# Layer 1 attention rewritten in unrolled slots with one rounding pass, the mask added by TensorE, maxima and differences taken from PSUM

## The reference

```python
def _dyn_quant(x):
    s = jnp.maximum(jnp.max(jnp.abs(x), axis=-1, keepdims=True) / 127.0, EPS)
    q = jnp.clip(jnp.round(x / s), -127.0, 127.0)
    return (q, s)
def _w8a8_linear(x, w, b):
    qx, sx = _dyn_quant(x)
    qw, sw = _quant_weight(w)
    y = jnp.einsum('bnc,oc->bno', qx, qw) * (sx * sw[:, 0])
    return y + b
...
q = _w8a8_linear(x, wq, bq).reshape(B, N, H, D).transpose(0, 2, 1, 3)
...
scores = jnp.einsum('bhnd,bhld->bhnl', q, k) * inv_sqrt_d + mask[:, None]
attn = jax.nn.softmax(scores, axis=-1)
o = jnp.einsum('bhnl,bhld->bhnd', attn, v)
return _w8a8_linear(o, wo, bo)
```

## Time and profile before

| | |
|---|---|
| median of 3 runs | 2271.92 us (2270.27 to 2276.45) |
| the profiled execution | 2274.25 us, its span 2272.5 us |
| layer 0, up to 1671 us | 74% of the span |
| layer 1: attention's setup | 1671.0 to 1720.4 |
| attention | 1720.4 to 1964.6 |
| setup of the feed-forward part | 1964.6 to 2030.6 |
| feed-forward part | 2030.6 to 2272.5 |
| busy over the span | PE 87%, DVE 51%, ACT 46%, POOL 44% |

### The profile page before, as it was taken

One profiled execution on the slowest core, in us unless ns is written; L12 is line 12 of the kernel. 1 busy time (PEld: TensorE's weight loads), 2 busy tenths in 40 slices (PEclk: granted clock), 3 DMA queues, 4 the chain that ended last, 5 costly groups with the idle time before them and its releaser, 6 DMA issues. The chain is left out here.

```text
span 2272.5 us, 29205 instructions
## 1 busy us (share of the span) xinstructions
PE 1969.8 (87%) x9812; PEld 1410.0 (62%) x9850; DVE 1150.6 (51%) x2272; ACT 1045.7 (46%) x2189; POOL 989.2 (44%) x902
## 2 busy tenths in 40 slices
PE   3799999999999999999989999899964677328998
PEld 2566666766666676667657777799943455323443
DVE  4344433444334444444444582333445998566886
ACT  2454444444544444544442111466612433457775
POOL 1644444434544435535311000688822555107774
PEclk9999999999999999999988999899976978659999
DMA  4100000000000000000031003588666000000000
GB/s 133 47 2 1 10 29 20 1 10 1 29 20 1 10 10 19 1 1 1 1 128 47 24 15 100 170 235 231 183 190 233 3 3 2 1 28 10 24 20 24
DMA packets 71074, 114.59 MB, mean 50 GB/s; under 512 B 7552, under 2 KB 35072, under 8 KB 70224
## 3 DMA queue, kind: packets, MB, share of 16 engines
q1 hardware_dynamic: 63760, 95.95, 12.6%
q0 software_dynamic: 7168, 16.78, 3.6%
HBM read 91.74 MB, written 22.02 MB: 50 GB/s over the span
## 5 line engine op out<-in xcount | busy, mean ns | idle before, releaser
L578 POOL TENSOR_TENSOR a_xcl<-xT,a_xch 128x512 fp32r<-128x512 f32 x64 | 82.5, 1289 | 477.5 <-ACT a_xch L447 477.5
L517 DVE TENSOR_REDUCE a_nmax<-a_S 128x1 f32<-128x192 f32 (+3 forms) x256 | 139.0, 553 | 255.2 <-PE a_S L653 252.7
L709 PE MATMUL a_A<-a_pT,a_vf 128*128 128x512 f32 (+1 forms) x448 | 234.9, 606 | 1.3 <-ACT a_pT L460 1.2
L652 PE MATMUL a_S<-a_kT,a_qT 128*128 128x288 f32 (+3 forms) x640 | 213.9, 433 | 3.0 <-ACT a_pr_even L450 1.7
L110 PE MATMUL a_A<-a_wlo,a_xch 128*128 128x512 f32 x256 | 152.6, 596 | 12.1 <-DVE a_qb L540 9.4
L450 ACT ACTIVATE a_pr_odd<-a_S,a_nmax 128x320 f32<-128x320 f32 (+1 forms) x128 | 80.9, 633 | 178.2 <-DVE a_nmax L517 176.5
L460 ACT ACTIVATE a_pT<-a_TR 128x512 f32<-128x512 f32 (+1 forms) x224 | 133.0, 594 | 61.8 <-PE a_TR L699 61.8
L652 PEld LDWEIGHTS a_S<-a_kT,a_qT 128*128 128x128 f32 x640 | 120.8, 192 | 55.1 <-issue 27.6
L450 ACT ACTIVATE a_pr_even<-a_S,a_nmax 128x192 f32<-128x192 f32 (+1 forms) x128 | 66.9, 525 | 154.3 <-DVE a_nmax L517 154.2
L671 PE MATMUL a_A<-a_wkv,xT 128*128 128x256 f32 x512 | 134.8, 386 | 0.6 <-DMA a_wkv<-in_L_xattn_wv_dram 0.6
L1308 POOL TENSOR_TENSOR e_wlo<-expert_raw,e_whi 128x1408 fp32r<-128x1408 f32 x32 | 103.5, 3255 | 68.3 <-ACT e_whi L1381 68.3
(11 more groups left out here) (370 smaller groups left out, 5186.2 us busy)
## 6 DMA issues: line engine op xcount, KB each, us to landing
ffn_raw<-in_L_ffn_w_dram SPq DMA_DIRECT2D x6, 2048.0 KB
expert_raw<-in_L_ffn_w_gate_dram SPq DMA_DIRECT2D x16, 704.0 KB
expert_raw<-in_L_ffn_w_up_dram SPq DMA_DIRECT2D x16, 704.0 KB
expert_raw<-in_L_ffn_w_down_dram SPq DMA_DIRECT2D x16, 512.0 KB
x_res<-in_x_dram SPq DMA_DIRECT2D x4, 1024.0 KB
a_raw<-in_L_xattn_wq_dram SPq DMA_DIRECT2D x4, 1024.0 KB
a_raw<-in_L_xattn_wo_dram SPq DMA_DIRECT2D x4, 1024.0 KB
xn_rows<-xg SPq DMA_DIRECT2D x16, 256.0 KB, 2.0
```

Source lines behind the costliest of these rows:

```text
L517: ve.tensor_reduce(nmax[:, s % 2, i:i + 1], pair(s, i), AX.X, ALU.max, negate=True).then_inc(s_max, 1)
L578: pool.tensor_tensor(xcl[:, t % 2], xT[:, :, tok(t)], xch[:, t % 2].bitcast(F32), ALU.subtract).then_inc(xlo_ready, 1)
L652: pe.matmul(bank[:, lo:hi], qT[:, t % 2, hq], kT[:, par(t), lo:hi], start=True, stop=hi < nk)
L709: last = pe.matmul(A[:, A_USE["V", t, 0][0]], vf[r, par(t), i], pT[r, i % 2], start=i == 0, stop=i == nkt - 1)
```

## The change

Four stages are touched.

**The attention** is written like the feed-forward part: every engine walks over 21 slots, fully unrolled, and in a slot does the steps of its order string, each for the tile of the slot plus a lead (`AHEAD`). Within the steps:

- The mask, loaded once in the setup, is added in PSUM by PE: behind each product with `kbd` comes one of the identity with the mask (S). DVE takes the 16 maxima from PSUM (M) and writes `p = SC - maximum` from PSUM (s); POOL no longer has a part in that.
- The row sums come out of the product with the values, since `vbd` has two columns of ones more (V, 66 columns for 64); DVE divides the 128 x 512 result instead of the 128 x 1024 probabilities (N).
- Scale and bias of q are applied by ACT as it copies the turned q (k, four instructions of 128x128); the row scale as it copies q out of PSUM (i).
- Rounding: ACT adds ROUND = 12582912 + 0x6600 as it scales and writes f32 (q, O). The low half of such a word is the f16 of 1536 + integer; PE turns those halves, at a step of two elements (T, U), and DVE subtracts 1536 (x, o).
- Normalisation isn't multiplied out: ACT subtracts the mean (c), and the scale of the row comes from maximum and root alone (m).
- The gate is multiplied into the scales (`gsw`) and the bias (`gbo`) in the setup; POOL adds the bias to `x` (B) and later the result (A).

**Its setup** has one DVE pass for rounding in place of two, and loads `bq`, `bo` and the mask (`mask`, 512 KB in rows of 256 bytes), all ahead of `x_res`; DVE waits for all of them before it writes `kbd`. **In the feed-forward setup** `w3` is loaded at the stage's start, no longer during the attention. **In the feed-forward stage** `xq` and `hq` are f32, and PE turns their low halves.

```diff
-MAGIC = 12582912.0
+BIG = 1536.0
+ROUND = 12582912.0 + 0x6600
+def low_half(ap):
+    return ap.bitcast(F16).rearrange("p (n two) -> p n two", two=2)[:, :, 0]
...
-                        quantise(ve, c, wi[:, w, o], raw[:, 2 + w, o], inv[:, w, o:o + 1], scratch[:]).then_inc(quant_ready, 1)
+                        ve.tensor_scalar(wi[:, w, o], raw[:, 2 + w, o], inv[:, w, o:o + 1], ROUND, ALU.mult, ALU.add).then_inc(quant_ready, 1)
...
+    PE_ORDER = "S0 U0 P0 Q0 P1 T0 Y0 V0 K0 V1"
+    ACT_ORDER = "q0 t0 i0 t1 c0 v0 k0 e0 O0"
+    DVE_ORDER = "b0 M0 o0 s0 x0 Y0 N0 m0"
+    POOL_ORDER = "B0 p0 A0"
+    AHEAD = {"PE": {"T": 2, "Q": 1, "K": 1, "S": 0, "P": -1, "V": -1, "U": -2, "Y": -2},
+             "ACT": {"c": 3, "v": 3, "q": 2, "i": 1, "k": 1, "e": 0, "t": -1, "O": -1},
+             "DVE": {"b": 3, "m": 3, "x": 2, "M": 0, "s": 0, "N": -1, "o": -2, "Y": -2},
+             "POOL": {"B": 2, "p": 3, "A": -2}}
+    def walk(engine, order, do):
+        for slot in range(-3, NT + 2):
...
+                    if name == "S":
+                        pe.wait_ge(q_copied, s + 1)
+                        if s > 0:
+                            pe.wait_ge(centred, s)
+                        for g in range(KD):
+                            pe.matmul(SC[:, 4 * g:4 * g + 4], qT[:, u, g], kbd[:, g, b], start=True, stop=False)
+                            last = pe.matmul(SC[:, 4 * g:4 * g + 4], ident[:], mask[:, s].unsqueeze(1).broadcast_to([P, 4, T]), start=False, stop=True)
+                        last.then_inc(sc_full, 1)
...
+                    if name == "M":
+                        ve.wait_ge(sc_full, s + 1)
+                        ve.tensor_reduce(pm[:, u], SC[:], AX.X, ALU.max).then_inc(max_ready, 1)
+                    if name == "s":
+                        ve.wait_ge(max_ready, s + 1)
...
+                        ve.tensor_tensor(p[:, u], SC[:], pm[:, u].unsqueeze(2).broadcast_to([P, H1, T]), ALU.subtract).then_inc(centred, 1)
...
+                    if name == "k":
+                        act.wait_ge(q_turned, s + 1)
...
+                        for g in range(KD):
+                            last = act.activation(qT[:, u, g], QT[:, g], ACT.Identity, bias=bq[:, g:g + 1], scale=sq[:, g:g + 1])
...
-        xq = s_.sb("xq", [P, 2, 2, D], F16)
+        xq = s_.sb("xq", [P, 2, 2, D])
...
-                            last = pe.transpose(bank[:, k * P:(k + 1) * P], hq[:, u, (8 * n + k) * P:(8 * n + k + 1) * P], ident_h[:])
+                            last = pe.transpose(bank[:, k * P:(k + 1) * P], low_half(hq[:, u, (8 * n + k) * P:(8 * n + k + 1) * P]), ident_h[:])
```

More of the change, by code:

```diff
@@ L1446, in _, with attention1_setup_stage @@
                         split_down(e + 1)
[L1449 to L1477, removed]
+def attention1_setup_stage(nc, ident, gates, ctx_in, wq_in, wk_in, bk_in, wv_in, bv_in, wo_in, bq_in, bo_in, mask_in, wT, sq, bq, gsw, gbo,
+                           mask, kbd, vbd, x, y_dram, added):
+    SCALE = float(np.float32(1.0 / np.sqrt(D1)))
     with ExitStack() as ctx:
@@ L1553, in _ @@
                 pe.wait_ge(diag_ready, 1)
[L1554 to L1559, removed]
+                pe.wait_ge(m_read, use - 1)
+                for o in range(KD):
+                    last = pe.matmul(M[:, use % 2, o * P:(o + 1) * P], ones[:], diag[:, o], start=True, stop=True)
+                last.then_inc(m_full, 1)
                 for w in range(2):
@@ L1584, in _ @@
                 pool.memset(vbd[:].rearrange("p b j n -> p (b j n)"), 0.0).then_inc(const_ready, 1)
+                pool.wait_ge(const_ready, 2)
+                for side in range(2):
+                    r = slice(side * T, (side + 1) * T)
+                    pool.memset(vbd[r, :, :, 2 * D1 + side], 1.0).then_inc(const_ready, 1)
             @block.vector
@@ L1751, in _ @@
+                walk("ACT", ACT_ORDER, do)
             @block.vector
@@ new lines, in turns, with qy_free @@
+                def turns(names):
+                    taken = []
+                    walk("PE", PE_ORDER, lambda name, n, s: taken.append((name, s)) if name in names else None)
+                    return {use: taken[n - 1] for n, use in enumerate(taken) if n > 0}
+                QY_LAST, TB_LAST = turns("QY"), turns("TU")
+                def qy_free(name, s):
+                    if (name, s) in QY_LAST:
+                        name, s = QY_LAST[name, s]
+                        pe.wait_ge(qs_ready if name == "Q" else y_ready, s + 1)
@@ L1914, in ffn1_setup_stage, with _ @@
         with nc.Block() as block:
+            @block.sync
+            def _(sp):
+                for half in range(2):
+                    o = slice(half * 2, half * 2 + 2)
+                    sp.dma_start(raw3[:].rearrange("p (o c) -> p o c", c=F1)[:, o],
+                                 w3_in.rearrange("(o p) c -> p o c", p=P)[:, o]).then_inc(loaded[2], 16)
             @block.scalar
```

483 lines of the change are left out of this document (250 added, 233 removed).

## The result

The changed kernel takes **2212.77 us** (median of 4 runs, 2211.03 to 2216.17), the kernel before 2272.34 beside it: ratio 0.9737, 95% interval 0.9719 to 0.9756. That is 59.6 us less, where 44 were forecast; the time lies in the range, 0.8 us above its low end of 2212. The profiled execution took 2211.03 us with a span of 2209.0, 63.5 under the span before.

The account below looks back on a forecast made before the run. DVE bounded an attention turn (12.6 of 13.2 us) and PE would become the bound. Attention 42 us less plus setup 2 less, feed-forward 0, makes 44 less: 2271.9 - 44 = 2228 us, range 2212 to 2260.

Parts of the forecast that it names:

- low end of 2212: Whole kernel: bottom of the forecast range, from a slot of 9.7 (12 less) and the setup at its best (4 less).
- Rival 2: Attention: a loop of waits through DVE and ACT sets the slot at 11.8 to 12, total 2244; chance 0.14.
- The slot: Attention's middle: PE's 10.1 us of work plus about 0.5 of waits, 10.6 us; ends 9.7 and 12.
- I take 10.1: PE's work in an attention slot, between 8.8 and 10.5: ten steps, each with up to 0.17 of pipe end.
- The wait for k: Attention: next S waits for ACT's four copies, 0.29 each, 1.15 together, covered only by V1 (1.0): 0.2 to 0.4 open.
- The rest of the stage: Attention: ramp 14, slots 0 and 1 12 and 10, slots 2 to 14 138, tile 15's S 4, tail 24; sum 202.
- Rival 1: Attention: PE keeps the earlier clock of 0.82, slot 12.8, stage 230, total 2256; chance 0.13.
- rival 4: Attention: PE, made the bound, runs mostly at half clock; at 0.65 slot 16.0, stage 272, total 2298; chance 0.07.
- break-even slot of 14.0: Attention: from this slot on, at a mean clock of 0.75, the stage is no shorter than before.
- The setup: Attention's setup: 2.6 and 0.7 less, against 1.3 of DMA wait ahead of `kbd` (between 0 and 4): 2 us less.
- `w3`: Feed-forward setup: the load takes 13.4 us, first touched 28.8 us after its start, so hidden: 0.
- the strided halves: Feed-forward stage: step of two costs 0 to 0.055 us each, taken as 0; at f32's rate total 2253, chance 0.10.

Follow-up runs that it names:

- 5: Changed kernel with the mask products of S made twice: slot 11.75 us, median 2244.53 us, ratio 0.9866 to the kernel before.
- 2: Changed kernel with PE's step that turns q moved one place earlier, ahead of the first value product: slot 9.27 us, median 2205.21 us, ratio 0.9690 to before.
- 3: Changed kernel without the four mask products of S, so the mask isn't added: slot 9.22 us, median 2201.48 us, ratio 0.9673 to before.
- 4: Changed kernel with PE's turn of q one place earlier and DVE's statistics b one slot sooner: slot 9.17 us, median 2204.54 us, ratio 0.9692 to before.
- K: The changed kernel itself, against the kernel before: slot 10.02 us, median 2212.77 us, ratio 0.9737.
- experiment 6: Changed kernel with DVE taking the maxima three times, PE's work unaltered: slot 13.75 us, median 2272.60 us, ratio 0.9997 to before.
- 12: Kernel before with only the feed-forward stage's part of the change (f32 `xq` and `hq`, low halves turned): ratio 1.0010, stage 242.4 us.
- experiment 1: Changed kernel run once more, nothing altered: slot 10.02 us, median 2215.33 us, ratio 0.9732 to the kernel before.
- experiment 8: Changed kernel with the mask added by DVE and PE's four identity products gone: slot 10.51 us, median 2218.25 us, ratio 0.9757 to before.

## Why the prediction was right, and by how much it was off

**The mechanism held.** DVE bounded a turn, its work fell, and PE became the bound, with one wait of its own, that for `a_qT`, on top. Both halves of that sentence were tested: adding to S costs in full (5), and moving step K takes the wait away (2). What I had not seen is how close the next bound lay: DVE's chain of 9.2 to 9.3 us (2, 3) stands right behind the 10.02. Rival 2 named it, and put it at 11.8 to 12, over two microseconds too long; it doesn't bind as the change is written, where M still waits 0.24 for S, and binds as soon as PE gets shorter (2, 3).

**The slot was mis-sized, 10.6 for 10.02.** The mis-sized term is "I take 10.1, since about half of the steps follow a wait that has to end first". PE's work is 9.13 us (10.02 less the 0.89 that its loads wait), and 9.17 with nothing between (4). One step of the ten has a wait on its row, S. The others queue behind one another with a few tenths lost at P1 and Y, and the end of the pipe that a row's length holds lies beside the next step: S costs 1807.30 - 1803.74 = 3.56 for the 4.0 that I had, Y 0.86 for 1.02, V0 0.84 for 1.0. I had that number, 0.17 a step, and the low bound of 8.8 that it gives, and chose a place near the far end. The sum should have started from 8.8, with an end added only where a wait is certain. The Trainium skill (TensorE: Matmul & The Clock Gate, Part 2, the step-by-step on what each phase is for) says that the drain of one matmul overlaps the fill of the next; these rows agree.

**The wait for k, 0.75 to 0.89 for 0.5.** Each of the four instructions of 128 columns took 0.46 us, all four 1.50; I had 0.29 each and 1.15, "near the one of few columns". The error is of the other sign and takes back some 0.4 of the 1.0 above. Both bounds, 0.28 and 0.60, held it, and the middle would have been better than an end.

**The rest of the stage**, predicted and measured: ramp 14 and 11.95 (1725.00 - 1713.05); slots 0 and 1 together 22 and 18.6, since PE was back at the full clock within the first score step (its pairs of products take 1.06 us up to the one at 1728.57, 0.59 from 1730.01 on) and not after the second slot; 13 slots 138 and 130.2; S of tile 15 with the tail 28 and 26.0. In all 202 and 186.8. Half of the 15 us lies in the slot, the other half in three pieces that were each taken a little long.

**DVE and ACT.** The sum for DVE was 8.4 busy, and the window gives 30.55 / 4 = 7.6. The copies cost 0.41 for 0.36, but the small instructions are seven and not nine, 1.35 for 1.7, the division 0.69 for 0.75, and neighbours overlap by some tenths in all. ACT was put at 6.8 and has 6.65. Neither matters for the time here; DVE's does for the next bound.

**The clock, rivals 1 and 4.** In the middle it was 1.00, above the 0.95 that I named. Rival 1 has lost: the 0.82 of before did not carry over. The kernel before has one long idle piece in each turn, ahead of P; these are two turns of it:

```profile
1791.51 1.97 PE L1834 MATMUL a_PT<-ident_f,a_p 128*128 128x128 f32 x8 [3.02 <-POOL a_p L1708]
...
1804.67 1.09 PE L1834 MATMUL a_PT<-ident_f,a_p 128*128 128x128 f32 x8 [1.76 <-POOL a_p L1708]
```

Behind 3.02 us without work the same eight products take 1.97 us, and behind 1.76 they take 1.09; all five turns of its middle with 3.02 or 3.03 are slow behind it, and those with 1.92 and less are not; between these, one with 2.45 is slow and one with 2.79 isn't. In K the longest piece is 0.9. The mechanism of rival 4 is real, and experiment 6 reached it from the other side: idle in one piece for 2.19 us, PE lost half its clock in the loop, slot 13.75, attention 245.4 us for 244.1 before, ratio 0.9997. That is nearly the break-even slot of 14.0 that the prediction gave. But it takes a late DVE to make it.

The Trainium skill (TensorE: Matmul & The Clock Gate, Part 4) states that PE's full clock doesn't engage for transposes and that they don't count as busy in the same way. This profile speaks against it. In the attention some 2 us of each slot are transposes (U, P0, P1, T and K, five of its ten steps), at a clock of 1.00. And in the feed-forward setup, where PE has next to nothing but transposes, the full clock came behind a row of them:

```profile
1917.56 3.51 PE L2053 MATMUL t_TR<-t_ident_b,t_tern 128*128 128x128 bf16 x32
1921.95 1.07 PE L2053 MATMUL t_TR<-t_ident_b,t_tern 128*128 128x128 bf16 x16 [0.88 <-DVE t_tern L2020]
```

The next sixteen, behind 2.52 us without work, took 1.89 again.

**The setup, 2 us forecast and 2.2 measured, with two terms off that cancel.** From `kbd` on the gain is 2.5 where 3.3 were expected; the DMA wait that I put at 1.3 is not there: `kbd` comes 262.4 us after the mark in the expert stage for 262.0 before.

**`w3` costs nothing that the rows show, and the strided halves cost a microsecond or two at most, as far as the profiles show**, for 0 forecast: no wait ahead of `t_junk`, eight halves in 0.61 us, loads of 99 ns packed or strided, and a stage 0.6 to 2.1 us longer (12), for a reason that stays open. The Trainium skill (TensorE: Matmul & The Clock Gate, Weight-path perf modes) has 16-bit weights keep the fast load when they are strided; the loads of 99 ns agree.

**The sum.** Of the 63.5 us in the span, 57.3 are the attention (42 forecast), 2.2 the setup (2), and 5.2 scatter in layer 0, which experiment 1 exposes; without them the change is worth 58 us, and the medians say 59.6 and 58.5. That the time is still in the range is in part luck. The low end of 2212 was built from a slot of 9.7 and a setup at its best, and neither came: it was a slot of 10.02, and a ramp, first slots and tail that were each shorter than I had taken them.

## What to carry to other kernels

When an engine's steps queue back to back, price them from start to start, and add the end of the pipe only before a step whose wait is certain. Then write down the second bound too, as a chain that closes on itself (here N, m, b, M, o on DVE and T, Y, V0, K, V1 on PE), and check that each link really waits for the one ahead: what is taken from the first bound pays only down to the second, and an order string is best changed at the one step that stands queued in front of others while it waits. In a loop that runs through PE, idle time is dearer than its length once the clock falls, and work without a purpose put into it can make the kernel faster; that real work moved there does as much was not tried.

## What the runs showed that was not expected

- PE idle in one piece for 2.18 to 2.20 us a slot (experiment 6): the half clock behind it in eleven slots in a row, and a stage 21 us longer than with that piece filled by 1.7 us of needless products. But 2.66 us in one slot of the same run left the clock at 1.00. With 1.84 us in one piece (experiment 8) the middle stayed mostly at 1.00 and slipped once, to 12.14 us for one slot. In the kernels whose pieces in the middle are about 1.0 us or less, the clock from 1770 to 1850 was 1.00 throughout.
- ACT from PSUM: 128 columns with a scale and a bias per partition 0.46 us (L1748), against 0.60 for 512 columns without. Four small ones cost 1.50; one large one would cost about 0.6, an estimate from that row.
- The kernel before doesn't have one turn but several. From step y to step y its middle takes 13.07 to 13.46 us, and twice 14.3: in those two DVE waits 1.10 and 1.13 us for scores that PE makes at the half clock. So the turn of 13.1 that I started from is the one at which DVE alone is the bound, and the clock added to some of the others. That PE's long idle pieces brought the 0.82 is read from these rows; no run took them away.
